# Products of queries and state on eight TensorE tiles, with centred first pairs and new engine orders

## The chip, the cores and the metric

One core of a Trainium2 chip runs the whole program in one launch. The metric is the device time of that core in microseconds (us). TensorE (PE) multiplies matrices into PSUM, VectorE (DVE) and ScalarE (ACT) work on PSUM and SBUF, GpSimd (POOL) on SBUF alone, and SyncE (SP) issues most DMAs. Each engine runs its own list of instructions in program order and waits on semaphores.

## The reference

The input x is (2, 1024, 128) in float32. It goes through one layer of retention (attention with decay) and one mixture of experts, each behind a layer norm and with a residual:

```
xn = layernorm(x)
q, k = rotary(xn Wq^T), rotary(xn Wk^T)      4 heads of 32
v, g = xn Wv^T, xn Wg^T                      4 heads of 64
o[t] = sum over s <= t of decay[h]^(t-s) * (q[t] . k[s]) / sqrt(32) * v[s]
x = x + (rmsnorm(o) * w * silu(g)) Wo^T
xn = layernorm(x)
x = x + sum over the top 2 of 8 experts of weight * ffn_e(xn) + shared_ffn(xn)
```

## The kernel before

**Tiles.** The 1024 positions are cut into 8 chunks of 128, and both sequences are worked on together: a *pair* (g, p) is one chunk of both, two tiles of 128 rows. Two pairs make a group g of four tiles (512 rows). Retention is done by pairs with a state S that is carried from chunk to chunk; the experts are done by groups, on transposed data of 128 features by 512 rows.

**Retention of a pair.** `stats1` and `normalize1` (DVE) or `x1_norm` (ACT) make the layer norm, with the reciprocal deviation `RS1` from POOL (`rstd1`: add, then power). `NORM1` is the number of pairs that DVE normalises. `x1_t` transposes on PE. The transposed data are split into a high part (`x1_hi`, ACT) and a low part (`x1_lo`, DVE), and each projection is three products of high and low parts of data and weights (`proj_qk`, `proj_v`, `proj_g`); the weights' low part comes from `low_w`, 256 columns for q and k on DVE, 512 for v and g on POOL. `rotary` multiplies q and k with cosine and sine tables (three DVE instructions), `rotate` adds the two parts, on POOL for the first four pairs and on DVE for the rest. `qk_t` transposes, `scores` makes the 128 by 128 products per head, `masked` (DVE) applies the decay, `state_add` and `state` carry S on. `attend` adds two products for each head and sequence in PSUM: queries times S (line 1129, from the second pair on; 32 rows of one head times 128 columns, 64 moving columns), and the masked scores times the values (line 1135, already in two halves of 64 columns). A product in float32 shows as two matmul instructions in the profile. `squares`, `mean_squares`, `rms`, `gate_out`, `normalize_out`, `out_t` and `proj_out` finish the layer; `add_attention`, `stats2` and what follows prepare the second norm.

**Experts of a group.** `router`, `route_a`, `rank`, `exps`, `route_b` and `comb_t` find the weights of the top 2; the rows are spread to all partitions by a DMA through DRAM (`widen`). `up_proj(g, k)` makes the hidden layer of expert k, `hidden` (ACT) its silu, `gating` (DVE) multiplies it with the weight, and `down_proj` adds up the experts in bank Y. The last group is mixed on DVE instead (`down_last`, `mix`).

**What sets the order.** The lists at the end of each engine's block are written out step by step. `after(signal, g, n)` in PE's list makes PE wait until a bank is free again. `PLACE` says which PSUM bank a step of a pair uses where that isn't the bank in `OWN`. `keep_busy` are products of the identity with itself ahead of the first work.

Of the kernel before, what the change touches and what calls it, by code (L numbers as in the profile page):

```python
# [42 lines left out]
NORM1, NORM2 = 4, 4  # L43
# [51 lines left out]
def retention_moe_kernel(nc, x, wqkvg, wot, gnw, upw, upb, dnw, dnb, gatew, const, rotary_tables, scratch, out):  # L95
    ctx = ExitStack()
    with ctx:
# [163 lines left out]
        def _(sp):  # L261
# [8 lines left out]
            sp.dma_start(W[:, QK:], wqkvg[:, QK:]).then_inc(ld_w[1].sem, 16)  # L270
# [58 lines left out]
        def _(pool):  # L329
# [64 lines left out]
            low_w(1)  # L394
# [13 lines left out]
            normalize_out(0, 0)  # L408
            rms(0, 1)
            normalize_out(0, 1)  # L410
            rstd2(0, 0)
            rms(1, 0)
            rstd2(0, 1)
            normalize_out(1, 0)
# [3 lines left out]
            rms(2, 0)  # L418
            rstd2(1, 1)
            normalize_out(2, 0)  # L420
# [6 lines left out]
            rms(3, 1)  # L427
            rstd2(3, 0)
            normalize_out(3, 1)
# [3 lines left out]
        def _(act):  # L433
            load_first_x(act, 1)
            act.dma_start(W[:, 0:QK], wqkvg[:, 0:QK]).then_inc(ld_w[0].sem, 16)

# [3 lines left out]
            def x1_norm(g, p):  # L440
                act.wait_ge(nm1.sem, pair(g, p) - NORM1 + 1)
# [10 lines left out]
            def values(g, p):  # L452
                act.wait_ge(v_ps.sem, v_ps.at(g, p))
                act.copy(V[:, slot(g, p)].rearrange("r b n -> r (b n)"), place("proj_v", g, p)).then_inc(v_sb.sem, 1)

            def gates(g, p):
# [3 lines left out]
                act.activation(SG[:, slot(g, p)].rearrange("r b n -> r (b n)"), place("proj_g", g, p), ACT.Silu).then_inc(sg.sem, 1)  # L460
# [77 lines left out]
            split_w(0)  # L538
            split_w(1)
            x1_hi(0, 0)  # L540
            x1_hi(0, 1)
            gates(0, 0)
            split_experts()
            gates(0, 1)
            values(0, 0)
            x1_hi(1, 0)
            values(0, 1)
            x1_hi(1, 1)
            split_biases()
            qk_sb(0, 0)  # L550
            gates(1, 0)
            gates(1, 1)
            qk_sb(0, 1)
            squares(0, 0)
            x1_norm(2, 0)
            values(1, 0)
            values(1, 1)
            x1_hi(2, 0)
            qk_sb(1, 0)
            qk_sb(1, 1)  # L560
            x1_norm(2, 1)
            x1_norm(3, 0)
            gates(2, 0)
            x1_hi(2, 1)
            squares(0, 1)
            transposed_out(0, 0)
            x1_norm(3, 1)
            gates(2, 1)
            qk_sb(2, 0)
            values(2, 0)  # L570
            transposed_out(0, 1)
            squares(1, 0)
            x2_hi(0, 0)
            values(2, 1)
# [3 lines left out]
            gates(3, 0)  # L578
            x2_hi(0, 1)
# [4 lines left out]
            exps(0)  # L584
            transposed_out(1, 1)
            hidden(0, 0)
            hidden(0, 1)
            squares(2, 0)
            comb_rows(0)
            comb_sb(0)  # L590
            gates(3, 1)
            hidden(0, 2)
            x2_hi(1, 0)
            hidden(0, 3)
            values(3, 1)
            squares(2, 1)
            x2_hi(1, 1)
            qk_sb(3, 1)
            transposed_out(2, 0)
            hidden(0, 4)  # L600
            exps(1)
            transposed_out(2, 1)
            squares(3, 0)
            hidden(0, 5)
            hidden(0, 6)
            x2_norm(2, 0)
            hidden(0, 7)
            comb_rows(1)
            comb_sb(1)
            hidden(0, 8)  # L610
            x2_norm(2, 1)
            x2_hi(2, 0)
            hidden(1, 0)
            transposed_out(3, 0)
            squares(3, 1)
            hidden(1, 1)
            x2_hi(2, 1)
            hidden(1, 2)
            x2_norm(3, 0)
            sums(0)  # L620
            transposed_out(3, 1)
            exps(2)
            hidden(1, 3)
            hidden(1, 4)
            hidden(1, 5)
            x2_norm(3, 1)
            comb_rows(2)
            hidden(1, 6)
# [3 lines left out]
            hidden(2, 0)  # L632
            x2_hi(3, 0)
            x2_hi(3, 1)
            hidden(2, 1)
            sums(1)
            hidden(2, 2)
            hidden(2, 3)
            exps(3)
            hidden(2, 4)  # L640
            hidden(2, 5)
            hidden(2, 6)
            comb_sb(3)
            hidden(2, 7)
            hidden(2, 8)
            hidden(3, 0)
            hidden(3, 1)
            sums(2)
            hidden(3, 2)
            hidden(3, 3)  # L650
            hidden(3, 4)
            hidden(3, 5)
# [5 lines left out]
        def _(dve):  # L658
# [27 lines left out]

            def x1_bias(g, p):
# [10 lines left out]
            def rotary(g, p):  # L698
                dve.wait_ge(qk.sem, qk.at(g, p))
                dve.wait_ge(ld_rot[pair(g, p)].sem, 16)  # L700
                if pair(g, p) >= 2:
# [4 lines left out]
                dve.tensor_tensor(RA[:, p], src.rearrange("r (b n) -> r b n", b=2), cos.unsqueeze(1).to_broadcast([P, 2, QK]),  # L706
                                  ALU.mult)
# [6 lines left out]
            def rotate(g, p):  # L714
                dve.wait_ge(rparts.sem, rparts.at(g, p))
                dve.tensor_tensor(QKR[:, slot(g, p)].rearrange("r b n -> r (b n)"), RA[:, p].rearrange("r b n -> r (b n)"),
# [181 lines left out]
            stats1(0, 0)  # L898
            stats1(0, 1)
            low_w(0)  # L900
            normalize1(0, 0)
            normalize1(0, 1)
            x1_lo(0, 0)
            stats1(1, 0)
            x1_lo(0, 1)
            stats1(1, 1)
            rotary(0, 0)
            normalize1(1, 0)
            normalize1(1, 1)
            rotary(0, 1)  # L910
            x1_lo(1, 0)
            stats1(2, 0)
            x1_lo(1, 1)
            state(0, 0)
# [634 lines left out]
```

## Time and profile before

| | |
|---|---|
| median of three runs | 142.51 us (142.03 to 142.53) |
| profiled execution | 142.45 us |
| its span, first to last instruction | 140.7 us |
| PE, DVE, ACT, POOL busy | 93%, 74%, 56%, 35% of the span |
| mean granted clock of TensorE | 0.988 of full speed |

Busy time of an engine is the time in which it has an instruction under way; since matmuls overlap, a busy PE is not PE at its peak. Times of single steps are given from the start of the span.

### The profile page before, as it was taken

What the parts mean: (1) busy time and instruction counts of PE and PEld (TensorE: products, weight loads), DVE (VectorE), ACT (ScalarE), POOL (GpSimd) and SP (SyncE); (2) the same over time, 40 slices, a digit from 0 to 9 for tenths busy, and PEclk for the clock granted to TensorE, in tenths of its full rate; (3) what the DMA queues carried; (4) which work ended last, traced back from release to release, by engine and by line L of the source; (5) the groups of instructions that cost most, each with busy time, mean ns of one, the idle gap of its engine ahead of it and who ended that gap; (6) DMA issues with size and microseconds to landing.
All of it is one profiled execution on the core that took longest, in us unless ns stands there. A gap on an engine that the chain in (4) does not pass through costs nothing.

```text
span 140.7 us, 3363 instructions
## 1 busy us (share of the span) xinstructions
PE 130.8 (93%) x1249; PEld 103.7 (74%) x1249; DVE 104.2 (74%) x311; ACT 78.6 (56%) x138; POOL 48.8 (35%) x69
## 2 busy tenths in 40 slices
PE   5659899899999999999998999999999999999990
PEld 5549799798978988886885675776557655589990
DVE  3589999989689997998796949679443982113983
ACT  4223937955562478555659762697745864471130
POOL 5458897937372342815222804502000000000000
PEclk9977999999999999999999999999999999999999
DMA  4999910000000000097000097010197200002002
GB/s 113 296 274 317 334 68 0 5 0 5 0 5 0 2 5 0 17 320 270 2 5 0 16 317 270 2 56 19 47 276 283 75 2 0 0 0 79 0 0 75
DMA packets 8659, 12.50 MB, mean 89 GB/s; under 512 B 1298, under 2 KB 5676, under 8 KB 8644
## 3 DMA queue, kind: packets, MB, share of 16 engines
q1 hardware_dynamic: 8356, 12.10, 26.7%
q8 instruction: 10, 0.16, 0.5%
q10 hardware_dynamic: 288, 0.20, 0.4%
q14 instruction: 5, 0.04, 0.1%
HBM read 11.20 MB, written 1.10 MB: 87 GB/s over the span
## 4 chain that ended last, share of the span: by engine, by line
PE 72%; DVE 10%; DMA 5%; SPq 4%; ACT 3%; issue 3%; DVEq 0%
PE bY L1238 17%; PE bU L1061 8%; PE bU L1062 7%; PE bU L1063 7%; DMA UW<-upw 5%; PE bA L1135 5%; PE bA L1211 4%; PE bU L1154 3%; PE bA L1129 3%; PE bA L1105 2%; PE bM L1154 2%; PE bU L1145 2%; PE bM L1180 1%; DVE SC L724 1%; SPq L267 1%
## 5 line engine op out<-in xcount | busy, mean ns | idle before, releaser
L497 ACT ACTIVATE HB<-bU,UB 128x512 f32<-128x512 f32 x36 | 24.3, 686 | 22.0 <-PE bU L1063 21.7
L1238 PE MATMUL bY<-HG,DW 128*128 128x512 f32 x48 | 24.5, 594 | 0.0
L848 DVE TENSOR_TENSOR HG<-CB,HB 128x512 f32<-128x512 f32 x24 | 16.3, 688 | 10.9 <-ACT HB L497 10.2
L353 POOL TENSOR_TENSOR RR<-SS,NHALF 128x8 f32<-128x8 f32 x8 | 13.5, 1684 | 25.9 <-DVE SS L743 25.9
L1061 PE MATMUL bU<-XH,UWH 128*128 128x512 f32 x36 | 21.5, 597 | 0.0
L1062 PE MATMUL bU<-XL,UWH 128*128 128x512 f32 x36 | 14.2, 395 | 0.0
L1063 PE MATMUL bU<-XH,UWL 128*128 128x512 f32 x36 | 14.2, 393 | 0.0
L1061 PEld LDWEIGHTS bU<-XH,UWH 128*128 128x128 f32 x36 | 6.8, 189 | 5.5 <-issue 4.3
L1238 PEld LDWEIGHTS bY<-HG,DW 128*128 128x128 f32 x48 | 8.4, 190 | 2.5 <-issue 1.4
L724 DVE TENSOR_TENSOR SC<-bA,MASK 128x512 f32<-128x512 f32 x16 | 10.2, 679 | 0.0
L1062 PEld LDWEIGHTS bU<-XL,UWH 128*128 128x128 f32 x36 | 6.8, 190 | 3.4 <-issue 3.4
L472 ACT ACTIVATE SQ<-bA 128x512 f32<-128x512 f32 x8 | 4.8, 598 | 8.1 <-PE bA L1135 8.1
L1135 PE MATMUL bA<-V,SC 128*64 128x64 f32 x256 | 9.2, 225 | 0.0
L1135 PEld LDWEIGHTS bA<-V,SC 128*64 128x64 f32 x256 | 8.1, 138 | 0.6
L360 POOL TENSOR_TENSOR OG<-OGR,RR 128x512 f32<-128x512 f32 x8 | 8.4, 1049 | 0.2
L1211 PE MATMUL bA<-DW,HB 128*128 128x128 f32 x64 | 8.2, 277 | 0.0
L1211 PEld LDWEIGHTS bA<-DW,HB 128*128 128x128 f32 x64 | 7.8, 191 | 0.3
L1061 PE MATMUL bU<-WH,XH 128*128 128x256 f32 x26 | 7.8, 301 | 0.2 <-DVE XL L695 0.2
L1063 PEld LDWEIGHTS bU<-XH,UWL 128*128 128x128 f32 x36 | 6.8, 188 | 1.6
L886 DVE SCALAR_TENSOR_TENSOR YS<-bA,CMB,YS 128x128 f32<-128x128 f32 x28 | 7.4, 344 | 0.5 <-PE bA L1211 0.5
L1062 PE MATMUL bU<-WL,XH 128*128 128x256 f32 x26 | 7.3, 279 | 0.0
L1063 PE MATMUL bU<-WH,XL 128*128 128x256 f32 x26 | 7.3, 279 | 0.0
(180 smaller groups left out, 317.8 us busy)
## 6 DMA issues: line engine op xcount, KB each, us to landing
CB<-scratch SPq DMA_DIRECT2D x12, 512.0 KB, 5.8
ROT<-rotary_tables SPq DMA_DIRECT2D x8, 256.0 KB, 4.5
out<-OUT SPq DMA_DIRECT2D x8, 128.0 KB, 1.8
X<-x SPq DMA_DIRECT2D x7, 128.0 KB, 6.1
UW<-upw SPq DMA_DIRECT2D x1, 576.0 KB, 6.6
DW<-dnw SPq DMA_DIRECT2D x1, 576.0 KB, 5.5
W<-wqkvg SPq DMA_DIRECT2D x1, 256.0 KB, 3.7
W<-wqkvg ACTq DMA_DIRECT2D x1, 128.0 KB, 3.9
```

Of the source, the lines that this page charges most:

```text
L353: pool.tensor_tensor(RR[:, n], SS[:, n], NHALF[:, 0:2 * H], ALU.pow).then_inc(rr.sem, 1)
L360: pool.tensor_tensor(OG[:, p].rearrange("r (n v) -> r n v", v=DV), OGR[:, p].rearrange("r (n v) -> r n v", v=DV), RR[:, pair(g, p)].unsque ...
L497: act.activation(HB[:, k, :], bU[(g * (E + 1) + k) % 2][:, :], ACT.Silu, bias=UB[:, e:e + 1]).then_inc(hid.sem, 1)
L724: last = dve.tensor_tensor(SC[:, p, h:h + 2], bA[:, h:h + 2, 0:2 * P].rearrange("r h (b n) -> r h b n", b=2), MASK[:, h:h + 2, :].unsqueez ...
L848: dve.tensor_tensor(HG[:, k % RING, :], CB[:, k - 1, :], HB[:, k, :], ALU.mult).then_inc(gated.sem, 1)
L886: done = dve.scalar_tensor_tensor(out=dst, in0=src, scalar=CMB[:, m, k - 1:k], in1=YS[:, t], op0=ALU.mult, op1=ALU.add)
L1061: pe.matmul(out_, ah, bh, start=start, stop=False)
L1062: pe.matmul(out_, ah, bl, start=False, stop=False)
L1063: return pe.matmul(out_, al, bh, start=False, stop=stop)
L1135: last = pe.matmul(bA[q, h, b * DV:(b + 1) * DV], SC[:, p, h, b, q], V[:, slot(g, p), b, h * DV:(h + 1) * DV], start=(n == 0 and b == 0), ...
L1211: last = pe.matmul(dst, HB[:, k, t], DW[:, e * P:(e + 1) * P], start=first, stop=final)
L1238: pe.matmul(bY[:, :], DW[:, e * P:(e + 1) * P], HB[:, 0, :] if k == 0 else HG[:, k % RING, :], start=(k == 0), stop=(k == E)).then_inc(dow ...
```

## The change

- **State products** (line 1129): the 128 columns of a head's queries are cut in two halves of 64, each written to its 64 partitions of PSUM. A product uses 32 rows by 64 columns of the array, so the four heads and two halves take eight different tiles, and there are twice as many instructions.
- **Centred first pairs**: for the first two pairs (`FOLD = 2`) DVE only subtracts the mean (`center1`). The factor `RS1` is applied behind the projections: in `values` and `gates` as the scale of an activation, one for each half, in `rotary` and `rotate` as a scalar of DVE instructions, one for each half. The third and fourth pair are normalised on ACT (`NORM1` is 2).
- **Engines**: all rotations and both `low_w` are now DVE's. The second part of W is loaded from ACT's queue, behind the first; the constants are loaded behind the fourth X.
- **Orders and places**: the lists of all engines, the banks and the waits on them are laid out anew.

```diff
-NORM1, NORM2 = 4, 4
+NORM1, NORM2 = 2, 4
+FOLD = 2
...
             load_first_x(sp, 0)
-            sp.dma_start(W[:, QK:], wqkvg[:, QK:]).then_inc(ld_w[1].sem, 16)
             load_x(sp, 1)
...
+            load_x(sp, 3)
             sp.dma_start(CN[:, :], const).then_inc(ld_c.sem, 16)
-            load_x(sp, 3)
...
             rstd1(0, 0)
             rstd1(0, 1)
-            low_w(1)
             rstd1(1, 0)
             rstd1(1, 1)
             fold_norm()
-            rotate(0, 0)
             low_experts()
-            rotate(0, 1)
             rstd1(2, 0)
             rstd1(2, 1)
-            rotate(1, 0)
-            rotate(1, 1)
+            rms(0, 0)
+            normalize_out(0, 0)
             rstd1(3, 0)
-            rms(0, 0)
...
             act.dma_start(W[:, 0:QK], wqkvg[:, 0:QK]).then_inc(ld_w[0].sem, 16)
+            act.dma_start(W[:, QK:], wqkvg[:, QK:]).then_inc(ld_w[1].sem, 16)
...
             def gates(g, p):
...
+                if pair(g, p) < FOLD:
+                    act.wait_ge(rs1.sem, rs1.at(g, p))
+                    for b in range(2):
+                        last = act.activation(SG[:, slot(g, p), b], place("proj_g", g, p)[:, b * HV:(b + 1) * HV], ACT.Silu,
+                                              scale=RS1[:, 2 * pair(g, p) + b:2 * pair(g, p) + b + 1])
...
+            def center1(g, p):
+                dve.wait_ge(mv1.sem, mv1.at(g, p))
+                for b in range(2):
+                    t = g * TILES + 2 * p + b
+                    last = dve.tensor_scalar(XN1[:, g % 2, (2 * p + b) * P:(2 * p + b + 1) * P], X[:, t * P:(t + 1) * P],
+                                             MV1[:, t, 0:1], None, ALU.subtract)
+                last.then_inc(xn1.sem, 1)
...
             def rotate(g, p):
                 dve.wait_ge(rparts.sem, rparts.at(g, p))
+                if pair(g, p) < FOLD:
+                    for b in range(2):
+                        t = 2 * pair(g, p) + b
+                        last = dve.scalar_tensor_tensor(out=QKR[:, slot(g, p), b], in0=RB[:, p, b], scalar=RS1[:, t:t + 1],
+                                                        in1=RA[:, p, b], op0=ALU.mult, op1=ALU.add)
...
             def attend(g, p):
...
-                            pe.matmul(bA[:, h, b * DV:(b + 1) * DV], QKT[r, slot(g, p), 0, b, :], S[r, n % 4, b * DV:(b + 1) * DV],
-                                      start=(b == 0), stop=False)
+                            for half in range(2):
+                                q = slice(half * (P // 2), (half + 1) * (P // 2))
+                                pe.matmul(bA[q, h, b * DV:(b + 1) * DV], QKT[r, slot(g, p), 0, b, q],
+                                          S[r, n % 4, b * DV:(b + 1) * DV], start=(b == 0), stop=False)
```

The new lists begin and, for the last group's attention, run on like this ([..] is an after-wait on a bank; only its signal is given):

```
DVE   stats1(0,0) center1(0,0) stats1(0,1) center1(0,1) low_w(0) x1_lo(0,0) low_w(1) stats1(1,0) x1_lo(0,1)
      rotary(0,0) x1_bias(1,0) stats1(1,1) rotate(0,0) rotary(0,1) state(0,0) rotate(0,1) x1_lo(1,0) x1_bias(1,1)
      stats1(2,0) masked(0,0) stats1(2,1) rotary(1,0) x1_lo(1,1) rotate(1,0) mean_squares(0,0) gate_out(0,0) ...
ACT   split_w(0) x1_hi(0,0) split_w(1) x1_hi(0,1) values(0,0) gates(0,0) x1_norm(1,0) gates(0,1) values(0,1)
      qk_sb(0,0) x1_hi(1,0) split_experts x1_norm(1,1) qk_sb(0,1) gates(1,0) ...
PE    keep_busy(7) x1_t(0,0) keep_busy(2) x1_t(0,1) proj_qk(0,0) proj_v(0,0) proj_g(0,0) proj_qk(0,1)
      [rparts] proj_g(0,1) [v_sb] proj_v(0,1) qk_t(0,0) [sg] state_add(0,0) x1_t(1,0) [sg] scores(0,0) [st] qk_t(0,1)
      [rparts] proj_g(1,0) [v_sb] proj_qk(1,0) [qkt] x1_t(1,1) attend(0,0) [sg] proj_v(1,0) [rparts] state_add(0,1)
      proj_v(1,1) [v_sb] qk_t(1,0) state_add(1,0) [ogr] scores(0,1) ...
      up_proj(2,3) proj_out(3,0) proj_out(3,1) y_t(1) up_proj(2,4) state_add(3,1) up_proj(2,5) down_proj(2,0)
      up_proj(2,6) down_proj(2,1) x2_t(3,0) down_proj(2,2) x2_t(3,1) down_proj(2,3) up_proj(2,7) down_proj(2,4)
      up_proj(2,8) down_proj(2,5) router(3) up_proj(3,0) down_proj(2,6) up_proj(3,1) down_proj(2,7) up_proj(3,2)
      down_proj(2,8) up_proj(3,3) up_proj(3,4) y_t(2) comb_t(3) up_proj(3,5) down_last(3,0) ...
```

## Rows read from the trace of the kernel before

**Rows 1.** The page: busy time, share of the span and instructions of each engine.

```profile
PE 130.8 (93%) x1249; PEld 103.7 (74%) x1249; DVE 104.2 (74%) x311; ACT 78.6 (56%) x138; POOL 48.8 (35%) x69
```

**Rows 2.** Timeline, 3 to 9.4 us: start, duration, engine, line, operation, [idle before <-releaser].

```profile
3.61 0.25 DVE L676 BATCH_NORM_AGGREGATE MV<-ST 128x2 f32<-128x6 f32 x2
5.44 0.49 DVE L672 BATCH_NORM_STATS2 ST<-X 128x6 f32<-128x128 f32 x2 [1.58 <-DMA X<-x]
6.44 0.60 DVE L683 TENSOR_SCALAR XN<-X,MV,RS 128x128 f32<-128x128 f32 x2
7.43 1.54 DVE L683 TENSOR_SCALAR XN<-X,MV,RS 128x128 f32<-128x128 f32 x2 [0.40 <-POOL RS L348]
9.36 0.57 PE L1061 MATMUL bA<-WH,XH 128*128 128x256 f32 x1
```

**Rows 3.** Windows: stretch, length, busy PE, PEld, DVE, ACT, POOL, PEclk, DMA.

```profile
5.00:10.00 5.00, 2.22 (x13) 1.75 (x13) 4.07 (x14) 1.55 (x4) 2.25 (x3) 0.86 1.01 285
10.00:15.00 5.00, 5.00 (x37) 5.00 (x36) 4.82 (x13) 2.12 (x5) 3.90 (x7) 0.80 0.98 314
```

**Rows 4.** Timeline, 11 to 18 us, DVE and POOL.

```profile
11.17 0.66 DVE L706 TENSOR_TENSOR RA<-bA,ROT 128x512 f32<-128x512 f32 x1
12.40 2.16 DVE L683 TENSOR_SCALAR XN<-X,MV,RS 128x128 f32<-128x128 f32 x4
13.09 1.40 POOL L389 TENSOR_TENSOR QKR<-RA,RB 128x512 f32<-128x512 f32 x1
...
15.08 2.65 POOL L374 TENSOR_TENSOR UWL<-UW,UWH 128x1152 fp32r<-128x1152 f32 x1
```

**Rows 5.** Groups by line: out<-in, count, busy us, mean ns, idle before.

```profile
L716 DVE TENSOR_TENSOR QKR<-RA,RB 128x512 f32<-128x512 f32 x4 | 2.7, 673 | 0.0
```

**Rows 6.** Chain that ended last, 59 to 63 us: start, us on it, what.

```profile
59.66 0.36 PE bM L1115 x16
...
61.61 0.60 PE bA L1129 x16
62.21 1.08 PE bA L1135 x32
```

**Rows 7.** Windows of weight loads alone, lines 1129, then 1135: (x) counts those under way.

```profile
61.53:61.64 0.11, 0.10 (x4) 1.00 1.06 298
61.64:61.75 0.11, 0.11 (x8) 1.00 0.59 224
...
62.13:62.19 0.06, 0.05 (x2) 1.00 0.83 341
62.19:62.25 0.06, 0.06 (x4) 1.00 0.67 273
```

**Rows 8.** Timeline of PE, 15 to 28 us.

```profile
15.66 0.60 PE L1097 MATMUL bA<-IDN,QKR 128*128 128x128 f32 x4
16.62 0.43 PE L1115 MATMUL bY<-V,QKR 128*32 128x64 f32 x16 [0.36 <-ACT V L454]
...
26.16 0.73 PE L1105 MATMUL bA<-QKT 32*128 32x128 f32 x16 [0.18 <-DVE OGR L750]
27.10 0.36 PE L1061 MATMUL bU<-WH,XH 128*128 128x256 f32 x1 [0.21 <-DVE XL L695]
```

**Rows 9.** Timeline of DVE, 48 to 55 us: routing's two parts, six and ten instructions.

```profile
48.58 0.21 DVE L793 TENSOR_REDUCE LG<-bM 128x32 f32<-128x64 f32 x1
...
50.07 0.42 DVE L809 TENSOR_REDUCE RANK<-BEF 128x32 f32<-128x256 f32 x1
...
52.94 0.15 DVE L815 TENSOR_REDUCE Z<-EX 128x4 f32<-128x32 f32 x1
...
54.48 0.19 DVE L837 TENSOR_TENSOR CX<-CMB,CX 128x32 f32<-128x32 f32 x1
```

**Rows 10.** Chain that ended last, 100 to 102 us.

```profile
100.03 0.86 PE bY L1238 x2
101.58 0.86 PE bY L1238 x2
```

More of the change, by code:

```diff
@@ L1304, in _ @@
+            after(ogt, 0, 0)
+            qk_t(1, 1)
+            after(xl1, 2, 0)
+            x1_t(2, 1)
+            after(sg, 1, 1)
+            proj_qk(2, 0)
+            after(ogr, 0, 1)
+            scores(1, 0)
+            after(qkt, 1, 1)
+            proj_v(2, 0)
+            after(sg, 2, 0)
+            proj_v(2, 1)
             after(rparts, 2, 0)
             proj_g(2, 1)
-            after(sg, 2, 0)
+            after(v_sb, 2, 0)
             proj_qk(2, 1)
-            proj_out(0, 0)
@@ L1309, in _ @@
-            after(ogr, 0, 1)
-            scores(1, 0)
+            attend(1, 0)
             after(sg, 2, 1)
+            out_t(0, 1)
+            after(rparts, 2, 1)
             qk_t(2, 0)
-            after(x1, 0, 0)
+            after(v_sb, 2, 1)
+            qk_t(2, 1)
+            after(ogt, 0, 1)
+            x1_t(3, 0)
+            after(xl1, 2, 1)
             state_add(1, 1)
-            after(rparts, 2, 1)
-            proj_v(2, 0)
             after(qkt, 2, 0)
-            out_t(0, 1)
@@ L1319, in _ @@
[L1319 to L1332 removed]
+            state_add(2, 0)
+            after(ogr, 1, 0)
+            scores(1, 1)
+            after(st, 2, 0)
@@ L1333, in _ @@
+            state_add(2, 1)
+            after(xl1, 3, 0)
             x1_t(3, 1)
             after(qkt, 2, 1)
-            state_add(2, 1)
-            after(ogr, 1, 0)
-            scores(1, 1)
-            after(xl1, 3, 0)
             proj_qk(3, 0)
+            after(st, 1, 1)
+            proj_out(0, 0)
             after(xl1, 3, 1)
-            proj_g(3, 0)
-            after(st, 2, 0)
+            proj_out(0, 1)
+            attend(1, 1)
+            after(x1, 0, 0)
+            out_t(1, 0)
@@ L1343, in _ @@
+            after(x1, 0, 1)
+            qk_t(3, 0)
+            after(st, 2, 1)
+            proj_v(3, 0)
+            proj_out(1, 0)
+            after(ogr, 1, 1)
+            scores(2, 0)
+            after(v_sb, 3, 0)
+            x2_t(0, 0)
+            after(qkt, 3, 0)
+            proj_v(3, 1)
+            after(x1, 1, 0)
             x2_t(0, 1)
-            attend(1, 1)
             after(rparts, 3, 0)
-            out_t(1, 0)
+            proj_qk(3, 1)
+            attend(2, 0)
             after(xl2, 0, 1)
@@ L1348, in _ @@
             router(0)
-            after(ogt, 1, 0)
-            qk_t(3, 0)
-            after(sg, 3, 0)
-            proj_v(3, 0)
-            after(ogr, 1, 1)
-            scores(2, 0)
-            after(qkt, 3, 0)
-            up_proj(0, 0)
-            after(v_sb, 3, 0)
-            proj_out(1, 0)
-            after(route_a_step, 0, 0)
-            out_t(1, 1)
-            after(st, 2, 1)
-            up_proj(0, 1)
-            attend(2, 0)
-            after(hid, 0, 0)
-            proj_out(1, 1)
@@ L1380, in _ @@
-            after(rparts, 3, 1)
-            up_proj(0, 3)
-            after(hid, 0, 2)
-            proj_v(3, 1)
-            attend(2, 1)
-            after(v_sb, 3, 1)
-            x2_t(1, 1)
-            after(xl2, 1, 0)
-            down_proj(0, 0)
+            proj_out(1, 1)
+            after(route_a_step, 0, 0)
+            x2_t(1, 0)
+            after(v_sb, 3, 1)
+            up_proj(0, 1)
+            attend(2, 1)
+            up_proj(0, 2)
+            after(hid, 0, 1)
+            out_t(2, 0)
@@ L1389, in _ @@
+            after(x1, 1, 1)
+            proj_g(3, 0)
+            after(hid, 0, 2)
+            proj_g(3, 1)
+            after(xl2, 1, 0)
+            comb_t(0)
+            after(ogt, 2, 0)
+            up_proj(0, 3)
+            after(ogr, 2, 1)
+            scores(3, 0)
+            after(ct_sb, 0)
+            x2_t(1, 1)
+            after(sg, 3, 1)
+            proj_out(2, 0)
             after(hid, 0, 3)
             qk_t(3, 1)
-            after(st, 3, 0)
-            out_t(2, 0)
-            down_proj(0, 1)
@@ L1394, in _ @@
-            after(xl2, 1, 1)
-            up_proj(0, 4)
-            after(ogt, 2, 0)
-            router(1)
-            after(ogr, 2, 1)
-            scores(3, 0)
-            after(hid, 0, 4)
-            proj_out(2, 0)
-            down_proj(0, 2)
-            after(route_a_step, 1, 0)
+            after(sg, 3, 0)
             out_t(2, 1)
             attend(3, 0)
+            after(x1, 2, 0)
+            up_proj(0, 4)
+            after(ogt, 2, 1)
+            state_add(3, 0)
+            after(xl2, 1, 1)
@@ L1406, in _ @@
+            router(1)
+            after(st, 3, 0)
+            down_proj(0, 0)
+            after(hid, 0, 4)
+            proj_out(2, 1)
+            down_proj(0, 1)
             after(qkt, 3, 1)
             up_proj(0, 5)
-            proj_out(2, 1)
-            after(x1, 2, 0)
+            down_proj(0, 2)
+            after(x1, 2, 1)
             up_proj(0, 6)
```

524 lines of the change are left out of this document (261 added, 263 removed), and 25 rows, old and new, of the table PLACE.

## The prediction

> **What bounds the kernel now.** I read the busy shares first, then the windows of the first 30 us, then the timeline of the start, and last the order in which TensorE's products begin. TensorE (PE) is busy 93% of the span [rows 1], and from its first projection at 9.36 [rows 2] it hardly stops: its queue is one list in program order, so the time is "when it starts, plus the work, plus its waits, plus what follows its last product". VectorE (DVE) comes next: in 10 to 15 us it is busy 4.82 of 5 us, and POOL 3.90 [rows 3]. So early on a wait of PE is nearly always a wait for DVE's list. What the change can win is thus the start, the waits, and the price of the products it cuts anew; the experts from about 100 us on stay PE's.
>
> The sum is made against the profiled execution, 142.45 us (span 140.7 and 1.7 around it); the median of the runs, 142.51, is the same within their spread.
>
> **The start.** Before, the first pair waits for its rstd from POOL. The DVE list, stats of pair 0, stats of pair 1, the low weights, then normalise, ends for the first pair at 7.04, and pair 1's normalise takes 1.54 instead of 0.60 [rows 2], so XL of pair 0 and the first projection come at 9.36. After, the pair is only centred, right behind its own statistics: 3.86 + 0.60 for two tiles = 4.5. The second X lands at 5.44 [rows 2]; its issue moves past the issue of W's second part (0.43 to 0.48 us on SP, which goes to ACT's queue, behind W's first part, where it delays only the warm-up activation). I take 4.9. Then stats 0.74 (5.65), centre 0.55 (6.2), low weights 0.31, x1_lo 0.34: the first projection can start at 6.9. That is 2.45 us earlier (1.9 if X lands no sooner than before). On SP the rotary tables and X move up with it, and the constants go behind the fourth X, 0.45 later, for a first use at about 13.6. proj_v now follows at once, and needs the low half of 512 columns of W, which moves from POOL to DVE, about 0.65 by the row of 512 columns [rows 5], done at 7.5; nothing waits long.
>
> **The half clock.** The granted clock was 0.86 in 5 to 10 and 0.80 in 10 to 15 us [rows 3]: 3.4 us at 1.2 GHz instead of 2.4, and PE's first products fall into it. About 2.6 us of them run at half speed, 1.3 us lost. After, PE has done more before that time (a projection and a half instead of two transposes), so the clock may not fall; if it falls at the same time, PE's work there has slack to DVE, and I charge 0.35. Gain 0.95 to 1.3; I take 0.95.
>
> **DVE's list to 21 us.** Removed: the normalising of four pairs, 0.60 + 1.54 + 2.16 = 4.3 [rows 2, 4]; 1.2 of centring comes for two of them, and the other two go to ScalarE, which also gets the first pairs' values and gates in halves, four activations more; it is busy 2.12 of 5 us there [rows 3]. Added: low weights 0.65; four rotations from POOL, 4 x 0.68 [rows 5]; about 0.6 for the first two rotary steps and rotations in halves with RS1; two small biases, 0.3. Net DVE +1.15 us, while POOL loses four rotations (1.40 the first [rows 4]) and a low_w. The 2.16 for four tiles stands beside POOL's rotation of 13.09 to 14.49, the 0.60 for two beside none [rows 2, 4]: part of the 4.3 was that collision, and it goes.
>
> I walk the new lists with start-to-start prices: stats 0.68, rotary 1.23 (11.17 to 12.40 [rows 4]), 1.45 in halves, rotation 0.8 in halves, x1_lo 0.34, mask 1.20. DVE: low weights to 7.5; stats(1,0) when its X has landed, to 8.7; x1_lo(0,1) 9.05; rotary(0,0) 10.5; bias and stats(1,1) 11.3; rotation(0,0) 12.1; rotary(0,1) 13.6; state, rotation(0,1) 14.65; x1_lo(1,0) 15.0; stats(2,0) 15.8; masks(0,0) 17.0; and so to 21.1 at the first gated output. PE then waits: proj_qk(0,1) for XL 0.2; proj_g(0,1), which takes the bank that rotary(0,0) reads, 9.8 to 10.55, 0.75; qk_t(0,0) for the rotation 0.25; scores(0,0) for QKT 0.25; qk_t(0,1) for the second rotation, 14.15 to 14.8, 0.65; attend(0,0) 0.15; scores(0,1) and small ones 0.4. Sum 2.65. Behind each stand the next group's projections in PE's one queue, and with them DVE's next rotary. Before has in the same stretch about 1.2: 0.36 ahead of the state_add of 16.62, 0.18 and 0.21 ahead of the products of 26.16 and 27.10 [rows 8], and smaller ones. So +1.45. The low bound is no more waits than before (+0), the high one that DVE's added 1.15 is paid in full once more (+2.6).
>
> **The state products.** Per pair with a state, 16 instructions of 32 rows by 128 columns with 64 moving columns take 0.60 us in the chain, the 32 of SC x V in 128 by 64 take 1.08, and 16 of 128 by 32 take 0.36 [rows 6]. The loads show why: with four tiles four begin, and the next four 0.11 later; with two tiles of 64 columns two begin, and the next two 0.06 later [rows 7]. A round lasts as the weights' columns do, 128 or 64, and holds as many instructions as there are tiles. The change halves the columns, doubles the tiles and the instructions: 4 rounds, as before, of 0.06 instead of 0.11. With the entry unchanged, 0.60 - 3 x 0.05 + 0.02 = 0.47. Bounds: below, 0.36 as the 16 of 128 by 32; above, 32 at today's 0.0375 each, 1.20, if tiles of one row group don't run beside each other. The nearest row is that of 128 by 64 (same columns, same moving side, and its two column tiles do run together), so 0.47: 7 x -0.13 = -0.9; ends -1.7 and +4.2.
>
> The row of 128 by 32 shows 16 starts in 0.36 us, entry and all, 22.5 ns each [rows 6]. The Trainium skill ("TensorE: Matmul & The Clock Gate", section "Wait — 56ns, not 53.3ns?") says that starts never come closer than about 25 ns however small the product. By that the 32 would take 0.80, and the change would cost 7 x 0.20 = 1.4 instead of giving 0.9; the trace stays under that figure already, but only for 16 in a row.
>
> **Order and places.** New banks and the after-waits on them cost nothing by themselves; the warm-up products move to bank A3 as Y is now used early. POOL, free of rotations, reaches rms(0,0) at once, and normalize_out no longer queues behind two rstd. Walked on to up_proj(0,5), with each of PE's steps at its smallest start-to-start time, the new lists come out 5.5 us ahead of before and show no larger wait; the smallest times flatter them by some 0.02 a step, 2 us over a hundred, so I keep to the sum by parts. Before has about 1.5 us of waits after 28 us, and I leave these unchanged. The last group's attention is put off: proj_out(3,0) goes behind up_proj(2,3), router(3) behind down_proj(2,5). Routing on DVE takes 1.9 + 1.7 us [rows 9]; a down_proj and an up_proj together take 1.55, the step between two down_proj of the chain, 0.86 of it the down_proj [rows 10]. Between router(3) and comb_t(3) PE has three such pairs and two more up_proj, 4.65 + 1.4 = 6.0, which hides the routing and the product that DVE has ahead of it, 0.7. Cost 0; without that cover up to 3.6.
>
> **Sum.** 142.45 - 2.45 - 0.95 + 1.45 - 0.9 = 139.6. With the walk's lead of 5.5 us kept whole, 137.0.
>
> **The rivals.**
> *Vector binds (0.15).* For: 4.82 of 5 us busy [rows 3] and net +1.15 on it; rotations have two operands in SBUF, as the small biases and normalisings that stretched beside POOL. If POOL's 2.65 us of low expert weights [rows 4] fall onto rotations, the lists slip by that: 139.6 + 2.65 = 142.2, no change. Against: by the walk POOL's piece falls beside stats, masks and rotary, which read PSUM or one tensor. The Trainium skill's "GPSIMD Engine Reference", section "Key points", says that GpSimd contends with VectorE instructions that have two SBUF inputs or a two-port mode; the 2.16 for four tiles agrees for the second kind.
> *Instructions come too slowly (0.12).* For: 64 loads and products in a burst, more than any row shows. At the 22.5 ns of [rows 6] a state product takes 0.72: 139.6 + 0.9 + 0.8 = 141.3. By the Trainium skill's 25 ns it would be 141.9.
> *Tiles of one row group take turns (0.08): slower.* Place: line 1129 in seven attends; price 1.20 instead of 0.60, so 140.5 + 4.2 = 144.7. It decides from 0.88 per product on (140.5 + 7 x 0.28 = 142.45). Against: the column tiles of 128 by 64 begin together [rows 7].
> *The late router shows (0.06).* Routing plus the table loads for its exps leave comb_t(3) and the mixing late by half of 3.6: 141.4.
> *A second half-clock stretch (0.05)* from the early gaps, as long as the first and in full work: +1.7, 141.3.
>
> **How the numbers follow.** The forecast has the remaining 0.54, own range 137.0 to 140.9. Half a per cent, 0.7 us, is about what a measurement here can tell, so faster is below 141.75 and slower above 143.15. Faster: 0.52 of the forecast, 0.11, 0.03, 0.04 and 0.05 of the rivals in the order instructions, router, clock, vector: 0.75. Slower: 0.08 and the far tails of vector and router, 0.11. Same: 0.14. The range 137.0 to 142.3 leaves out the slower rival, the upper part of the vector rival and a little of the best case, some 0.2.
>
> **What would show it.** First projection at about 6.9 instead of 9.36; PE waiting at the first qk_t's and proj_g(0,1); the timeline's row of line 1129's successor with 32 instructions in about 0.47 until the SC product; no normalising beside POOL; comb_t(3) without a wait ahead of it. The prediction is wrong if the first projection starts after 8.5, if the 32 take over 0.6, or if PE stands still for more than 4 us in 7 to 25.

## The result and the profile after

The changed kernel takes 136.39 us (median of 4 runs, 136.18 to 136.50) against 142.27 for the kernel before in the same series: ratio 0.9587, 95% interval 0.9556 to 0.9618. Its profiled execution took 136.48, span 134.7. The forecast was 139.6, range 137.0 to 142.3: the direction was right, the gain twice as large as forecast, and the time lies 0.6 us under the range.

The page after: busy time, share of the span and instructions of each engine, and the clock in 40 slices, to be held against [rows 1].

```profile
PE 128.8 (96%) x1359; PEld 101.7 (76%) x1359; DVE 102.9 (76%) x318; ACT 81.2 (60%) x146; POOL 43.6 (32%) x64
...
PEclk9999999999999999999999999999999999999998
```

Windows after, as [rows 3]: stretch, length, busy PE, PEld, DVE, ACT, POOL, clock, DMA.

```profile
5.00:10.00 5.00, 4.97 (x30) 4.27 (x29) 4.41 (x18) 2.20 (x7) 2.18 (x4) 1.00 1.06 357
10.00:15.00 5.00, 4.53 (x59) 3.66 (x58) 4.97 (x20) 4.96 (x13) 1.65 (x3) 1.00 1.05 327
```

PE is full where it was busy 2.22 of 5 us, and DVE, at 4.97 of 5, is fuller than before. The start, as [rows 2], first DVE, then PE:

```profile
3.82 0.48 DVE L705 TENSOR_SCALAR XN<-X,MV 128x128 f32<-128x128 f32 x2
4.83 0.49 DVE L686 BATCH_NORM_STATS2 ST<-X 128x6 f32<-128x128 f32 x2 [0.53 <-DMA X<-x]
...
6.37 0.42 DVE L717 TENSOR_TENSOR XL<-bU,XH 128x256 fp32r<-128x256 f32 x1
```

```profile
6.89 0.55 PE L1102 MATMUL bU<-WH,XH 128*128 128x256 f32 x1
7.24 0.41 PE L1103 MATMUL bU<-WL,XH 128*128 128x256 f32 x1
7.45 0.37 PE L1104 MATMUL bU<-WH,XL 128*128 128x256 f32 x1
...
7.77 0.28 PE L1103 MATMUL bU<-WL,XH 128*128 128x256 f32 x1
7.89 0.28 PE L1104 MATMUL bU<-WH,XL 128*128 128x256 f32 x1
```

The first projection stands at 6.89 (forecast 6.9). Products follow each other at 0.21 us until 7.5 and at 0.12 from then on. The kernel before has the same 0.21 where its granted clock was low [rows 3], so the half clock holds for half a projection here, though the windows read 1.00. The match to 0.01 us is luck: with the same first steps the first projection stood at 6.29 to 6.62 in the traces of seven other runs below, and at 8.73 and 8.99 in two with the old start. The step of 2.5 us is not luck. The chain, as [rows 6], and the weight loads of the same product:

```profile
52.23 0.42 PE bA L1172 x32
52.64 1.08 PE bA L1178 x32
```

```profile
52.16 0.35 PEld L1172 LDWEIGHTS bA<-S,QKT 32*64 32x64 f32 x32 [0.36 <-issue]
```

A state product takes 0.42 instead of 0.60. Last, what PE waited for from 30 us to the end (us, times, longest; waits above 0.15), before and then after:

```profile
PE bM L1180 <- DVE X L757: 0.5, 1, 0.5
PE bU L1154 <- ACT HB L497: 0.3, 1, 0.3
PE bU L1115 <- ACT QKT L464: 0.2, 1, 0.2
PE bA L1129 <- DVE SC L724: 0.2, 1, 0.2
```

```profile
PE bU L1102 <- ACT HB L509: 0.2, 1, 0.2
```

So the 6.0 us of span split into 2.5 of start (9.36 to 6.89), 7 x 0.18 = 1.3 of state products, 1.0 of waits after 30 us, and a remainder of 1.2 for the half clock and the waits before 30 us together. The view counts a wait from the modelled end of the product ahead, so the last two parts are good to a few tenths only. The first two projections are twelve products; the thirteenth begins here, before and then after:

```profile
12.06 0.28 PE L1061 MATMUL bU<-WH,XH 128*128 128x256 f32 x1
```

```profile
8.89 0.28 PE L1102 MATMUL bA<-WH,XH 128*128 128x256 f32 x1
```

They took 2.70 us before and 2.00 after. So some 0.7 of the remainder is the half clock, and some 0.5 is fewer waits before 30 us. My sum had a gain of 0.95 and a loss of 1.45 for these two, and nothing for the waits after 30.

### The profile page after: what moved, and what is told of

It reads as the page before. It is cut to its first block, busy times and chain, and to the rows that moved or that the text cites. A ratio compares the mean times of both kernels' runs of the same rounds, so it can differ in the third digit from the quotient of the medians.

```text
span 134.7 us, 3595 instructions
## 1 busy us (share of the span) xinstructions
PE 128.8 (96%) x1359; PEld 101.7 (76%) x1359; DVE 102.9 (76%) x318; ACT 81.2 (60%) x146; POOL 43.6 (32%) x64
## 4 chain that ended last, share of the span: by engine, by line
PE 81%; DVE 7%; ACT 4%; DMA 4%; issue 2%; ACTq 1%; DVEq 0%
PE bY L1281 16%; PE bU L1102 9%; PE bU L1104 8%; PE bU L1103 8%; PE bA L1178 6%; PE bA L1254 5%; DMA W<-wqkvg 4%; PE bU L1197 3%; PE bA L1146 2%; PE bA L1172 2%; PE bU L1138 2%; PE bY L1102 1%; PE bM L1215 1%; PE bM L1197 1%; PE bM L1217 1%
## 5 line engine op out<-in xcount | busy, mean ns | idle before, releaser
L884 DVE TENSOR_TENSOR HG<-CB,HB 128x512 f32<-128x512 f32 x24 | 16.9, 719 | 11.1 <-ACT HB L509 7.2
L1102 PE MATMUL bU<-XH,UWH 128*128 128x512 f32 x36 | 22.6, 628 | 0.2 <-ACT HB L509 0.2
L369 POOL TENSOR_SCALAR VE<-MV 128x2 f32<-128x2 f32 x8 | 2.2, 281 | 29.2 <-DVE MV L804 29.2
L1102 PE MATMUL bU<-WH,XH 128*128 128x256 f32 x28 | 9.0, 321 | 0.0
L1103 PE MATMUL bU<-WL,XH 128*128 128x256 f32 x28 | 7.9, 284 | 0.0
L1104 PE MATMUL bU<-WH,XL 128*128 128x256 f32 x28 | 7.9, 282 | 0.0
```

The costliest lines, as they stand in the source:

```text
L884: dve.tensor_tensor(HG[:, k % RING, :], CB[:, k - 1, :], HB[:, k, :], ALU.mult).then_inc(gated.sem, 1)
L1102: pe.matmul(out_, ah, bh, start=start, stop=False)
L1103: pe.matmul(out_, ah, bl, start=False, stop=False)
L1104: return pe.matmul(out_, al, bh, start=False, stop=stop)
```

## The experiments

Two theories at first. *Parts add*: each edit gives its own gain wherever it stands. *Lists*: a lead of PE is worth only what the next queue behind it lets through, so that the new orders make the gain. A third, *ACT's queue*, was formed on the way: a lead of PE only lengthens a wait of ACT for a DMA, and what PE needs next stands behind that wait in ACT's list. Ratios are to the kernel before, from runs on the same chip.

**The tiles alone, and all but the tiles.**

```diff
 kernel before:
-  pe.matmul(bA[:, h, ...], QKT[r, slot(g, p), 0, b, :], S[...], ...)
+  for half in range(2): ... pe.matmul(bA[q, h, ...], QKT[r, slot(g, p), 0, b, q], S[...], ...)
```

> The kernel before with the eight-tile state products alone, its orders and all else as they were. Theory 'parts add' (PE's one queue is the time, so what a part saves on it arrives): the product falls from 0.60 to 0.41 us until the first product of scores and values, as in the profile after, seven times, so 142.3 becomes about 141.0, ratio 0.991. Rival 'lists' (in the first 60 us Vector's and Scalar's lists set the pace and PE absorbs what it is given): most of it turns into waits ahead of the next step, 141.9 or more, ratio over 0.997.

0.9935 (0.9908 to 0.9962), 0.9 us. The other way round, the changed kernel with four tiles:

> The kernel after with the state products in four tiles again. Parts add: 7 x 0.19 = 1.3 us more, 136.4 becomes 137.7, ratio to the kernel before 0.968. Lists: under 0.5 us more, 136.9 at most, ratio under 0.962. Should the eight tiles be worth clearly more than 1.3 here, the products would gain from the new order too, which neither theory says.

0.9714 (0.9678 to 0.9750), 1.8 us above the changed kernel. In both traces each of the seven attends moves by 0.18 to 0.20 us. The tiles add, at 0.9 to 1.8 by the times, 1.3 by the trace.

**The half clock in the kernel before.**

```diff
             x1_t(0, 0)
+            keep_busy(4)
             x1_t(0, 1)
```

> The kernel before with four more products of the identity between the two first transposes, where PE stands idle anyway. If TensorE's clock then stays at 2.4 GHz from 8.7 to 12 us: parts add says the 1.3 us that the first two projections lost at half clock come back, 142.3 becomes 141.0, ratio 0.991; lists says PE only waits longer for Vector's rotary parts and the first transposed pair, at most 0.3 us, ratio over 0.997. If the clock falls as before, the run tells nothing of this and the time is the same.

Ratio 1.000 (0.9978 to 1.0022), though in the profiled execution the half clock ended inside the first projection. The four products put the first projection off to 9.71; after two projections PE is 0.3 us ahead (11.76 against 12.06), and 0.1 of it is left at x1_t(1,1). A lead that came by itself went the same way: in the run of the tiles alone the first projection stood 0.63 us earlier than in the kernel before (8.73), and 0.2 was left at the first scores. The reason stands in ACT's timeline of this run:

```profile
13.57 1.16 ACT L530 CAST UWH<-UW 128x1152 fp32r<-128x1152 f32 x1 [0.93 <-DMA UW<-upw]
14.63 0.59 ACT L460 ACTIVATE SG<-bU 128x512 f32<-128x512 f32 x1
```

and the same place in the kernel before:

```profile
13.68 1.16 ACT L530 CAST UWH<-UW 128x1152 fp32r<-128x1152 f32 x1 [0.74 <-DMA UW<-upw]
14.74 0.59 ACT L460 ACTIVATE SG<-bU 128x512 f32<-128x512 f32 x1
```

`split_experts` waits for the DMA of the first expert weights, and ACT's gates, values and high parts stand behind it. An earlier PE only lengthens this wait. The 75 runs of the kernel before that stand beside these experiments fit: 23 with a mean clock of 0.995 or more have the median 142.23, 47 with 0.98 to 0.99 have 142.15. Only the five below 0.98 are longer (142.78 to 143.49). This is the weaker sign, since a mean clock can leave a stretch out, as the last section shows.

**The first pairs normalised again, all else as changed.** `FOLD = 0`, and `normalize1` in place of `center1`.

> The kernel after without centring: the first two pairs are normalised on Vector behind POOL's reciprocal deviation, and rotary, rotations, values and gates of these pairs go without the factor, in one instruction again. Parts add: the first projection comes some 1.1 us later (POOL's 1.1 us for the deviation of each pair stands in the chain), and the time with it, 137.5, ratio 0.967. Lists: Vector is relieved by about 1.0 us by then (fewer halves), which pays the late start back by 25 us, 136.6, ratio 0.960.

0.9766 (0.9740 to 0.9792), 2.5 us above the changed kernel, more than either theory gave. PE's timeline:

```profile
8.85 0.55 PE L1102 MATMUL bU<-WH,XH 128*128 128x256 f32 x1
...
13.68 0.41 PE L1103 MATMUL bU<-WL,XH 128*128 128x256 f32 x1
13.90 0.41 PE L1104 MATMUL bU<-WH,XL 128*128 128x256 f32 x1
...
14.32 0.28 PE L1103 MATMUL bU<-WL,XH 128*128 128x256 f32 x1
```

The first projection comes 2.0 us later, and at 0.21 us a product four projections run at half clock; PE is 3.4 us behind by the first scores (17.03 against 13.65), and 3.3 arrive at the end of this execution, the longest of the six. Two executions of the changed kernel itself say the same: the first projection stood at 6.32 in one and at 6.89 in the other, and their spans were 134.1 and 134.7. So in the new orders a late start and the half clock pass through whole, where in the old ones the half clock was swallowed.

**Centring in the orders of before.** The new first-pair code, with its two rotations on DVE, in the old lists.

```diff
 NORM1, NORM2 = 4, 4
+FOLD = 2
 DVE:  stats1(0, 0)
+      center1(0, 0)
       stats1(0, 1)
+      center1(0, 1)
       low_w(0)
-      normalize1(0, 0) normalize1(0, 1)
 ...
       normalize1(1, 1)
+      rotate(0, 0)
       rotary(0, 1) x1_lo(1, 0)
+      rotate(0, 1)
 POOL:
-      rotate(0, 0)
       low_experts()
-      rotate(0, 1)
```

> The kernel before, with the first two pairs centred only (the factor behind the projections, as in the change) and their two rotations moved from POOL to DVE; four tiles, and all other orders and places, stay those of before. Parts add: the first projection comes at 7.4 to 7.5 instead of 9.36 (the second X still lands at 5.44), and the 1.9 us arrive at the end: 140.3 us, ratio 0.987; if the half-clock stretch is gone or lies elsewhere this may move by 1 us either way. Lists: in the orders of before DVE's list binds up to 21 us, so most of the lead is gone by the first scores, 141.5 or more, ratio above 0.995.

It is *slower* than before: 1.0193 (1.0162 to 1.0224). ACT, then PE:

```profile
13.75 1.15 ACT L544 CAST UWH<-UW 128x1152 fp32r<-128x1152 f32 x1 [3.37 <-DMA UW<-upw]
14.81 0.83 ACT L470 ACTIVATE SG<-bU,RS 128x256 f32<-128x256 f32 x2
```

```profile
15.70 0.44 PE L1107 MATMUL bU<-IDN,XN 128*128 128x128 f32 x2 [3.21 <-ACT SG L470]
...
18.91 0.41 PE L1100 MATMUL bU<-WL,XH 128*128 128x256 f32 x1
19.13 0.41 PE L1101 MATMUL bU<-WH,XL 128*128 128x256 f32 x1
```

PE starts 1.8 us earlier, then stands 3.2 us at x1_t(1,1), because ACT stands 3.4 for the DMA, and comes out of the gap at half clock: its next two projections take 1.6 us each. Neither theory had this; it gave the third, tested by one moved step:

```diff
 ACT:
-      split_experts()
       gates(0, 1) values(0, 0) x1_hi(1, 0) values(0, 1) x1_hi(1, 1)
+      split_experts()
       split_biases()
```

> As the run with centred first pairs in the orders of before, with one step moved: ScalarE splits the first expert weights (split_experts) behind x1_hi(1,1) instead of ahead of gates(0,1). ACT's queue holds the lead (new theory: in the orders of before ScalarE stands at 10.4 to 13.75 us for the DMA of these weights, and gates, values and the next pair's high parts stand behind it): the gap of 3.2 us and the second half-clock stretch go, and the 1.8 us of the start arrive: 140.4 us, ratio 0.987. DVE's list holds it as well: most of the lead is still gone by the first scores, 141.5 to 142.5, ratio 0.995 or more.

0.9883 (0.9858 to 0.9909), 140.45 us as expected: one step on ACT is worth 4.4 us here, and 1.7 of the start's 1.8 arrive. The same step without the early start:

> The kernel before with the same one step moved and nothing else. ACT's queue holds the lead: its 0.74 us of waiting for the DMA and the 1.16 us of the split no longer stand ahead of the gates, values and high parts; TensorE's gaps of 0.4 to 0.6 us at x1_t(1,1) and state_add(0,0) shrink, 0.4 to 1.0 us less than before, ratio 0.993 to 0.997. DVE's list holds it: within 0.3 us of before, ratio 0.998 to 1.002.

1.0060 (1.0023 to 1.0098): no gain, and some 0.9 us more; this part of the theory fell. ACT's wait is gone, but POOL's `low_experts` follows the split, and the second rotation stands behind it in POOL's queue (17.69 before, [rows 4] show the piece ahead of it). The second qk_t needs this rotation and begins at 21.11 instead of 20.75; its row names ACT's gates, for which that step doesn't wait in PE's list:

```profile
17.07 2.66 POOL L374 TENSOR_TENSOR UWL<-UW,UWH 128x1152 fp32r<-128x1152 f32 x1
19.70 1.27 POOL L389 TENSOR_TENSOR QKR<-RA,RB 128x512 f32<-128x512 f32 x1
...
21.11 0.63 PE L1097 MATMUL bU<-IDN,QKR 128*128 128x128 f32 x4 [0.70 <-ACT SG L460]
```

Not every execution loses. Of the twelve, three with a mean clock of 0.999 or 1.000 took 142.1 to 142.2 us, as before; seven with 0.986 to 0.988, the profiled one among them, took 143.3 to 143.9, and two were longer still. So by these runs, once ACT's wait is out of the way, the half clock costs some 1.4 us that it didn't cost in the orders of before.

And the step moved the wrong way in the changed kernel, behind gates(0,0):

> The changed kernel with that step moved the other way: split_experts behind gates(0,0), ahead of the next pair's normalising, the other gates and values. The DMA lands at about 13.7 whatever the orders. ACT's queue: ScalarE stands from 10.7 to 13.7, gates(0,1) ends some 3.4 us later, TensorE has nothing for about 3 us and may fall to half clock: 139.0 or more, ratio above 0.976. If it is DVE's order that carries the lead, ScalarE has slack there: within 0.5 us of after, up to 137.0, ratio up to 0.962.

0.9886 (0.9845 to 0.9927), 140.3 us. The DMA landed earlier than I had said (11.3), so ACT's own wait was 0.94, but wait and split together put the second gates off by 1.7 us (13.18 against 11.46), PE stood 1.78 for them, and its clock fell (0.66 of full speed in 15 to 20 us). The mechanism held, the size of the wait did not.

```profile
11.34 1.16 ACT L542 CAST UWH<-UW 128x1152 fp32r<-128x1152 f32 x1 [0.94 <-DMA UW<-upw]
...
13.18 0.82 ACT L468 ACTIVATE SG<-bU,RS 128x256 f32<-128x256 f32 x2
```

Why the DMA landed at 11.3 there and at 13.6 to 13.75 in the runs above: a guess was the load of W's second part, which the change takes off SP's queue. That load put back, on top of the last kernel, and then alone in the changed kernel:

```diff
 SP:   load_first_x(sp, 0)
+      sp.dma_start(W[:, QK:], wqkvg[:, QK:])
       load_x(sp, 1)
 ACT:
-      act.dma_start(W[:, QK:], wqkvg[:, QK:])
```

> The changed kernel with split_experts behind gates(0,0) and the second part of W loaded from SP's queue again, behind the first X, as before. If the load's place sets when the first expert weights land: 13.6 us instead of 11.3, so ScalarE waits 2.3 us longer than the 0.94 without it, and the time rises by 2 us or more, 142 or above, ratio 0.998 or more. If the landing scatters from run to run: about as without it, 140.3, ratio 0.987.

> The changed kernel with only that load back on SP's queue. The second X is issued 0.48 us later and the first projection comes 0.4 to 0.5 later; the first expert weights are split at 13.75 in the changed kernel anyway, so their landing at 13.6 would not show. 0.4 to 0.6 us more than the changed kernel, 136.9, ratio 0.962 to 0.963. If W's second part landed earlier that way (its split waits 0.8 us for it in the changed kernel), no change: ratio 0.959.

0.9967 (0.9935 to 0.9999) and 0.9630 (0.9561 to 0.9700). In the first the weights land later, at 12.94, not at 13.6, and the run takes 1.1 us more than without the load, half of what was expected:

```profile
12.94 1.15 ACT L542 CAST UWH<-UW 128x1152 fp32r<-128x1152 f32 x1 [2.17 <-DMA UW<-upw]
```

Its first projection also stands 1.06 us later than in the run without (7.43 against 6.37), so the cost is not shown to be the landing's. Nor is it shown that this load's place sets the landing. From issue to landing the expert weights took 5.8 us in both runs with the load on SP's queue. They took 4.3 to 6.3 us in the ten runs whose loads are as in the changed kernel (4.8 there), and 6.0 to 6.7 in the seven in the orders of before. The change as a whole lands them sooner; what this one load gives is less than the spread.

Alone in the changed kernel the load's cost can't be told from none: the interval holds 0.9587. The trace shows the first projection at 7.43, 0.5 us later, as expected, and three projections at half clock behind it; there the split waits for nothing.

**Do the start and the tiles add?** The kernel with both moves in the old orders, and eight tiles:

> The orders of before with centred first pairs, the split of the expert weights moved back on ScalarE, and the eight tiles. Start and state products add: 140.45 less 7 x 0.19 = 1.3, 139.1 us, ratio 0.979; what is then left to the changed kernel, some 2.7 us, is its other orders. If the tiles overlap with the start (the waits that a shorter state product uncovers): 139.8 or more, ratio 0.984.

0.9824 (0.9777 to 0.9872), 139.5 us, between the two numbers; the interval holds both, so the times don't decide. By the trace each of the seven state products takes 0.42 us again. The changed kernel is 3 us below it. Waits of PE up to 30 us in this run:

```profile
PE bU L1099 <- DVE XL L717: 0.7, 1, 0.7
PE bA L1099 <- POOL WL L387: 0.4, 1, 0.4
PE bY L1153 <- ACT V L457: 0.4, 1, 0.4
PE bA L1099 <- DVE XL L717: 0.2, 1, 0.2
```

The same view of the changed kernel, where my text had 2.65 us:

```profile
PE bA L1146 <- ACT QKT L476: 0.3, 1, 0.3
PE bU L1138 <- DVE QKR L748: 0.2, 1, 0.2
```

The last row of the first list stands ahead of the first projection, which comes at 7.59, 0.7 us later than in the changed kernel. Behind it the early waits are 1.5 us against 0.5, and after 30 us the same four waits as before are 1.4 against 0.2. 0.7 + 1.0 + 1.2 is 2.9 of the 3.1 us between the spans, to a few tenths. It is read from traces; which single moves in the lists took each wait away was not tried.

**Single places.** `low_w(1)` back on POOL, behind rstd1(0,1):

> The changed kernel with the low half of the value and gate weights on POOL again, behind rstd1(0,1). It takes 0.61 us off DVE's list at 7.3 us; on POOL it took 1.26 us before, so it ends at about 8.5 instead of 7.96, while the first product with it stands at about 8.5. Vector binds: PE's early waits shrink with DVE's list, 0.4 to 0.6 us less than after, 135.9, ratio 0.955. Parts add: nothing waits for DVE there for long, within 0.2 us of after or up to 0.4 more through proj_v's wait, 136.3 to 136.8, ratio 0.959 to 0.962.

0.9641 (0.9599 to 0.9684), some 0.8 us worse. PE now waits for POOL's low weights. The profiled execution, 138.79, is the longest of the six (the others took 136.8 to 137.3), so its wait is more than the usual one:

```profile
9.38 0.55 PE L1102 MATMUL bY<-WH,XH 128*128 128x256 f32 x1 [1.90 <-POOL WL L387]
```

So no gain came of taking 0.61 us off DVE's list, but with POOL in the way this run can't show what the relief alone would be worth.

No `keep_busy` at all:

> The changed kernel without the products of the identity that keep TensorE busy ahead of its first work. The first projections then run at half clock, each group of three at 1.28 instead of 0.70 us. DVE covers it (as it covered the half clock before): at most 0.7 us more than after, 137.1 or less, ratio up to 0.964. The lead passes whole in the new orders: three to five groups at 0.58 each, 1.7 to 2.9 more, 138.1 to 139.3, ratio 0.971 to 0.979.

0.9619 (0.9580 to 0.9659), 137.4 us, with a wide spread (136.4 to 139.8): 0.5 us by the ratio, 1.0 by the medians. In its trace two and a half projections instead of half a one are at half clock, fewer than I had reckoned. PE is 1.1 us behind at the first qk_t, and 0.9 of that arrives at the end.

**The wait that is left.** After `router(3)` ACT loads two tables around `exps(3)`, 1.28 us each, and up_proj(3,3), which needs the hidden layer behind them, begins 0.8 us late (the view above, which counts from the modelled end of the product ahead, lists 0.2):

```profile
113.63 1.28 ACT L513 ACT_TABLE_LOAD   x1
114.93 0.23 ACT L513 ACTIVATE EX<-SHI 128x32 f32<-128x32 f32 x1
115.18 1.28 ACT L509 ACT_TABLE_LOAD   x1
116.47 1.27 ACT L509 ACTIVATE HB<-bU,UB 128x512 f32<-128x512 f32 x2
```

```diff
 PE:   up_proj(2, 8)
-      down_proj(2, 5)
       router(3) up_proj(3, 0)
+      down_proj(2, 5)
       down_proj(2, 6)
 DVE:
-      gating(2, 8)
       route_a(3) rank(3)
+      gating(2, 8)
```

> The changed kernel with one more down product behind the last router: router(3) goes ahead of down_proj(2,5), and on DVE gating(2,8) goes behind rank(3). In the trace after, up_proj(3,3) waits 0.8 us for hidden(3,1), which stands behind the two table loads around exps(3). If that wait is all that is lost there, 0.8 us less than after: 135.6 us, ratio to before 0.9535. If the wait only moves on to the mixing of the last group, no change: 136.4, ratio 0.959.

0.9556 (0.9527 to 0.9585). With down_proj(2,4) moved as well:

> The changed kernel with two more down products behind the last router (down_proj(2,4) and down_proj(2,5)). With one moved, the wait of 0.8 us at up_proj(3,3) was gone and 0.33 came back at up_proj(3,4). If that remainder goes as well: 0.8 us less than after, 135.6, ratio 0.953. If it only moves on again: as with one, 135.9 to 136.1, ratio 0.956.

0.9569 (0.9536 to 0.9602). Then beside the changed kernel on one chip:

> The changed kernel once more, beside the next one: 136.4, ratio 0.959.

> The changed kernel with two more down products behind the last router once more, beside the changed kernel itself on the same chip. By the trace, 0.78 us of waiting at up_proj(3,3) is gone: 0.5 to 0.9 us less than the changed kernel. If the difference was one of chips: within 0.3 of it.

0.9593 (0.9558 to 0.9628) and 0.9578 (0.9545 to 0.9610), 136.56 and 136.43 us: no difference that can be told. In the traces the stretch from up_proj(2,7) to up_proj(3,4) takes 0.4 us less (9.62 instead of 10.02, second product to second product), half of the 0.8, so the late begin was not all loss; and the start hides even that. The second part of W was split at 6.03 in the changed kernel's profiled execution and at 7.02 in the other, where the first qk_t came 1.0 us later:

```profile
6.03 0.62 ACT L536 CAST WH<-W 128x512 fp32r<-128x512 f32 x1 [0.33 <-DMA W<-wqkvg]
```

```profile
7.02 0.62 ACT L536 CAST WH<-W 128x512 fp32r<-128x512 f32 x1 [1.35 <-DMA W<-wqkvg]
```

A kernel faster than the changed one is not shown.

## Why the prediction missed, point by point

- **Start, 2.45: right in size.** It was 2.5; with the load of W's second part back on SP's queue the first projection stood at 7.43, so some 0.5 of it comes with that load. What I did not see is its condition: in the old orders the centred pairs make the kernel 2.7 us slower, and `split_experts` has to stand later on ACT for them to be a gain. The wait for its DMA stood in ACT's list before, and I read the list of DVE only.
- **Half clock, 0.95: about right, 0.7.** Here too I missed the condition. In the old orders it was worth nothing by itself (ratio 1.000), since ACT's wait for the DMA took up the time; it arrives only with the new orders.
- **Early waits, +1.45: the step that failed.** The term set 2.65 us of waits in the new orders against 1.2 before. The view lists 0.5 after, against the 0.75 of [rows 8]: the waits fell where I had them rise. The walk went wrong at two places above all. At proj_g(0,1) I had PE stand from 9.8 to 10.55. It was ready at 10.3, since it lost time at half clock in the first projection, which I had charged once already (0.35), and it began at 10.45. At the second qk_t I had it stand for 0.65, from 14.15 to 14.8; it stood for 0.17:

```profile
10.17 0.28 PE L1104 MATMUL bU<-WH,XL 128*128 128x256 f32 x1
10.45 0.39 PE L1102 MATMUL bU<-WH,XH 128*128 128x256 f32 x1
...
14.54 0.63 PE L1138 MATMUL bU<-IDN,QKR 128*128 128x128 f32 x4 [0.17 <-DVE QKR L748]
```

  DVE's steps from rotary(0,0) to the first gated output came 0.1 to 0.4 us earlier than the walk's prices had them. Half clock and early waits together were forecast at +0.5 and measured at -1.2. Of the 3.1 us between forecast and profiled execution, the early waits make some 2, the later waits 1.0 and the state products 0.4, less 0.25 of half clock. That the waits fell is read from the traces; which moves in the lists did it stays open.
- **"The smallest times flatter them by some 0.02 a step, 2 us over a hundred, so I keep to the sum by parts."** The walk of the new lists had said 5.5 us ahead at up_proj(0,5); that product began at 72.40 before and at 66.45 after, 5.95. The work ahead of it is nearly the same (a proj_out in place of a down_proj). The walk was 0.45 short, and the discount had no row behind it: with the lead kept whole the same text gives 137.0.
- **"Before has about 1.5 us of waits after 28 us, and I leave these unchanged."** Wrong by 1.0 as the view lists them: the new orders leave 0.2 of 1.2.
- **State products, 0.9: mechanism right, size too small.** 0.42, not 0.47: 1.3 in all. Windows of 0.055 us from the first load on show 8, then 16, then 24 loads under way, so a round holds eight, as reckoned. The two rivals on them fall. The loads of 32 instructions are issued in 0.35 us, 11 ns each. The Trainium skill ("TensorE: Matmul & The Clock Gate", section "Wait — 56ns, not 53.3ns?") gives some 25 ns as the closest that starts come; the trace disagrees, and the 32 take half of the 0.80 worked out from that figure.
- **Vector binds: fell.** DVE was as full as that rival said (4.97 of 5 us), but the slip did not come: POOL's low expert weights (15.18 to 17.85) fell beside masks, statistics and rotary, as the argument against it had said.
- **Late router: no cost from routing, a small one from its table loads**: a begin 0.8 us late, of which a shift gets back 0.4 in the traces and nothing that the times can tell.
- **A second half-clock stretch** did not come in the changed kernel; in four experiments a half-clock stretch came behind a gap of PE, of 1.8, 1.9, 3.1 and 3.2 us.

## What to carry to other kernels

When a start moves forward, look in every engine's list for the first step that waits for a DMA, and ask what stands behind it: the earlier start only lengthens that wait, and can end slower. Losses that run at the same time as such a wait (here the half clock) are not to be booked as gains of their own. The same holds within a sum: time that PE loses at half clock fills a wait behind it, and charging both counts it twice. Here one walk through the whole lists to a late step (5.5 against 5.95) was worth more than a sum of parts with waits from another walk in it (2.65 against 0.5), and what is taken off such a walk needs a row of its own.

## What the runs showed of the hardware that was not expected

- Eight tiles of 32 by 64 take 32 products in 0.42 us, where four tiles of 32 by 128 took 0.60 for 16.
- In the run with normalised first pairs the window of 10 to 15 us reads a clock of 1.00, while products stand 0.21 us apart until 14.1 and 0.12 apart after. There the spacing tells which clock it is, and that row does not:

```profile
10.00:15.00 5.00, 5.00 (x28) 5.00 (x27) 3.63 (x13) 1.95 (x4) 2.69 (x5) 1.00 1.07 326
```

- The same rotation took 0.87 us alone and 1.44 beside POOL's low expert weights (15.15 to 17.77), in the run with centred pairs in the old orders:

```profile
11.66 0.87 DVE L748 SCALAR_TENSOR_TENSOR QKR<-RB,RS,RA 128x256 f32<-128x256 f32 x2
...
17.01 1.44 DVE L748 SCALAR_TENSOR_TENSOR QKR<-RB,RS,RA 128x256 f32<-128x256 f32 x2
```

  The Trainium skill ("GPSIMD Engine Reference", section "Key points") says that POOL contends with VectorE instructions that read two tensors from SBUF; this row agrees. In the changed kernel that piece fell beside statistics, masks and rotary.
- The same load of 576 KB took 4.3 to 6.3 us from issue to landing in ten runs that issue their loads in one order, so a single trace's landing says little about an order of loads.
